# Last stage of a metaformer layer: the whole residual on VectorE, four statistics rows, weight pieces and centred gating weights

## The reference

```python
def conv(x, ...):                                  # x here is _ln_c(x)
    xn = layer_norm(x, norm_a, norm_b)
    left = (xn @ Wl + bl) * sigmoid(xn @ Wlg + blg)
    right = (xn @ Wr + br) * sigmoid(xn @ Wrg + brg)
    out_gate = sigmoid(xn @ Wog + bog)
    out = einsum('bkjd,bkid->bijd', left, right) / n
    out = layer_norm(out, on_a, on_b) * out_gate
    return out @ Wo + bo

def ffn(x, gate_w, gate_b, weight1, weight2):      # x here is _ln_t(t)
    logits = einsum('bsd,ed->bse', x, gate_w) + gate_b         # 64 experts
    probs = softmax(logits, axis=1)                            # over the tokens
    topv, topi = the 8 largest of each expert, and their tokens
    pooled = sum over the 8 of x[topi] * topv
    out = gelu([pooled, 1] @ weight1) then [., 1] @ weight2    # per expert
    return zeros.at[topi].add(out * topv)

x = x + conv(_ln_c(x), ...)
t = t + ffn(_ln_t(t), ...)
```

## Time and profile before

| | |
|---|---|
| median of 3 runs | 3088.07 us (3087.18 to 3091.25) |
| the profiled execution | 3078.97 us |
| its span in the profile | 3077.0 us |
| TensorE, VectorE, ScalarE, GpSimd busy over the span | 84%, 79%, 77%, 61% |
| last stage | about 1885 to 2953 us |

### The profile page before, as it was taken

How to read it: one execution, slowest core, us unless ns; L and a number is a source line. 1 busy time by engine, 2 the same in 40 slices (tenths; PEclk the granted TensorE clock), 3 DMA queues, 4 the chain that set the end, 5 groups by cost and what they waited for, 6 DMA issues and landing times.

```text
span 3077.0 us, 66113 instructions
## 1 busy us (share of the span) xinstructions
PE 2588.5 (84%) x14998; PEld 2145.9 (70%) x15070; DVE 2428.7 (79%) x4824; ACT 2363.5 (77%) x4284; POOL 1889.3 (61%) x2343
## 2 busy tenths in 40 slices
PE   7999999999999989989998984777777777777735
PEld 6888888888888878888988983555555555555523
DVE  6777777777777769999999996778777787787862
ACT  6888888888888877887878872888778787787850
POOL 8888888888888860000000003888788887887842
PEclk9999999999999999999999996999999999999967
DMA  5777777777777769999999985888888888888836
GB/s 199 270 267 268 267 270 273 270 269 269 267 268 268 270 256 318 333 327 325 343 330 325 332 295 185 301 309 307 297 300 309 303 299 298 309 309 297 303 139 202
DMA packets 281154, 873.00 MB, mean 284 GB/s; under 512 B 29223, under 2 KB 81602, under 8 KB 281122
## 3 DMA queue, kind: packets, MB, share of 16 engines
q1 hardware_dynamic: 272322, 855.31, 77.2%
q10 hardware_dynamic: 8448, 16.78, 1.6%
q0 software_dynamic: 352, 0.53, 0.2%
HBM read 492.97 MB, written 379.52 MB: 284 GB/s over the span
## 4 chain that ended last, share of the span: by engine, by line
PE 43%; DMA 17%; issue 14%; POOL 12%; DVE 5%; ACT 4%; SPq 2%; POOLq 1%; ACTq 0%; another core or an unknown queue 0%; DVEq 0%
PE banks L1267 32%; DMA arena<-left_d 11%; POOL rs L693 5%; DMA statrow<-stat_d 5%; POOL arena L664 4%; PE banks L1256 4%; PE banks L1335 3%; ACT arena L809 2%; PE banks L1301 1%; ACT work L879 1%; DVE left_parts L1006 1%; PE banks L1326 1%; PE banks L1336 1%; SPq L475 1%; DVE arena L1014 1%
## 5 line engine op out<-in xcount | busy, mean ns | idle before, releaser
L1267 PE MATMUL banks<-x_parts,w_parts 128*128 128x512 f32 x4320 | 1068.3, 399 | 0.8 <-POOL x_parts L626 0.8
L1267 PEld LDWEIGHTS banks<-x_parts,w_parts 128*128 128x128 f32 x4320 | 791.9, 189 | 162.9 <-POOL x_parts L626 1.2
L1301 PE MATMUL banks<-left_parts,right_parts 128*128 128x384 f32 x3456 | 629.3, 341 | 67.2 <-ACT arena L810 56.8
L1301 PEld LDWEIGHTS banks<-left_parts,right_parts 128*128 128x128 f32 x3456 | 606.2, 191 | 90.5 <-issue 86.0
L957 DVE SCALAR_TENSOR_TENSOR arena<-banks,cols,arena 128x512 f32<-128x512 f32 x576 | 406.6, 747 | 255.7 <-ACT arena L775 252.3
L879 ACT ACTIVATE work<-arena,nmr,rs 128x128 f32<-128x128 f32 x1152 | 458.9, 482 | 151.9 <-POOL nmr L695 145.5
L659 POOL COPY rcol<-late 128x8 f32 (+1 forms) x144 | 28.4, 197 | 722.3 <-ACT late L825 722.3
L664 POOL TENSOR_TENSOR arena<-arena,work 128x512 f32<-128x512 f32 x288 | 359.7, 1270 | 163.1 <-DVE arena L1063 161.9
L1335 PE MATMUL banks<-wo_sb,arena 128*128 128x128 f32 x2304 | 413.3, 309 | 0.1
L1335 PEld LDWEIGHTS banks<-wo_sb,arena 128*128 128x128 f32 x2304 | 373.6, 200 | 29.4 <-issue 1.8
L626 POOL TENSOR_TENSOR x_parts<-xn,x_parts 128x512 fp32r<-128x512 f32 x288 | 372.2, 1292 | 6.6 <-ACT x_parts L763 6.6
(11 more groups left out here) (177 smaller groups left out, 4459.5 us busy)
## 6 DMA issues: line engine op xcount, KB each, us to landing
arena<-in_x_dram SPq DMA_DIRECT2D x144, 512.0 KB, 3.4
left_d<-arena SPq DMA_DIRECT2D x144, 512.0 KB, 2.6
right_d<-arena SPq DMA_DIRECT2D x144, 512.0 KB, 3.4
gate_d<-arena SPq DMA_DIRECT2D x144, 512.0 KB, 4.2
arena<-right_d SPq DMA_DIRECT2D x128, 576.0 KB, 5.8
arena<-left_d SPq DMA_DIRECT2D x128, 576.0 KB, 6.8
mixed_d<-arena SPq DMA_DIRECT2D x128, 576.0 KB, 4.2
work<-mixed_d SPq DMA_DIRECT2D x144, 512.0 KB, 4.2
```

The lines of the kernel that those rows point to most:

```text
L1267: last = nc.tensor.matmul(ps[2 + k][:, :], w_parts[:, wq, k], x_parts[:, xq, b, c], start=((wq, xq) == TERMS[0]), stop=((wq, xq) == TERMS[ ...
L1301: last = nc.tensor.matmul(ps[NT * b + t][:, 0:GRID], lr_parts[RIGHT][:, rq, b, k, t * P:(t + 1) * P], lr_parts[LEFT][:, lq, b, k], start=( ...
```

## The change

- Residual: VectorE's `residual` now does both halves, eight operations. `scale_rest` on ScalarE and `residual_rest` on GpSimd are gone, with their semaphores; `store_result` waits for VectorE alone.
- Statistics rows: `statrow` loses its `b` dimension. A step's 18 rows lie at partitions 32r to 32r+17, r = s mod 4; `coef` is there four times. `outer` and `project` take these 18 partitions alone, with `tile_position=(BAND * r, 0)`. The loads run three steps ahead and wait for `project(s-4)` by their own step's number. SyncE and TensorE loop in fours (`quads`), and in SyncE's step the load of the statistics stands first.
- Weight pieces: `load_w1` issues one load of 0.5 MB at each of 28 cuts of ScalarE's loop, and four after it.
- Centred gating weights: each expert's mean over the channels is subtracted from `gate_nat` before the transpose. The logits then need no mean of the tokens: `normalise` becomes `x * rs`, and `minus` (L1092) and `nmr` (L695) go.
- Small ones: the sum of the exponents goes straight to `csum` (`keep_sum` is gone), `keep` copies two steps at once, and `exponentials` moves to the head of ScalarE's step.

The diff, cut:

```diff
+def quads(engine, steps, body, drain=0):
+
+    last = steps // 4 - 1
+    body(0)
+    with engine.Fori(1, last) as j:
+        body(j)
+    for j in range(last, steps // 4 + drain):
+        body(j)
...
-            def load_parts(i, b):
-                s = 2 * i + b
-                sp.wait_ge(s_z3, mark(2, s - 2, 2))
+            def load_parts(j, r):
+                s = 4 * j + r
+                if not isinstance(j, int) or j > 0:
+                    sp.wait_ge(s_z3, mark(2, s - 4, 2))
                 settle(sp, s_tick_sp)
-                sp.dma_start(statrow[0:KR, b], stat_r[s].broadcast_to([PARTS, 2 * PARTS, 2 * CHUNK])).then_inc(s_sin[b], 16)
+                sp.dma_start(statrow[BAND * r:BAND * r + KR], stat_r[s].broadcast_to([PARTS, 2 * PARTS, 2 * CHUNK])).then_inc(s_sin[r], 16)
...
-                        keep(*shifted(i, b, -4))
+                        if b:
+                            keep(i - 2)
...
-            def residual_rest(i, b):
-                pool.wait_ge(s_x3[b], 16 * (i + 1))
-                pool.wait_ge(s_zr, mark(1, 2 * i + b, 1))
-                half = late_arena[:, 1, b, 1]
-                nc.gpsimd.tensor_tensor(half, half, wv[:, 2, b, 1], ALU.add).then_inc(s_ra, 1)
...
             def load_w1(n):
-                for j in range(2 * n, 2 * n + 2):
-                    act.dma_start(w1_sb[:, j], w1_view[j]).then_inc(s_w1, 16)
+                j, first = n // 2, BANDS // 2 * (n % 2)
+                some = slice(first, first + BANDS // 2)
+                act.dma_start(w1_sb[:, j, some], w1_view[j, :, some]).then_inc(s_w1, 16)
...
-                        last = nc.scalar.activation(ys[:, b, h, c], summed[:, b, h, c], ACT.Identity,
-                                                    bias=nmr[:, b, k:k + 1], scale=rs[:, b, k:k + 1])
+                        last = nc.scalar.activation(ys[:, b, h, c], summed[:, b, h, c], ACT.Copy, scale=rs[:, b, k:k + 1])
...
-            cuts = [lambda n=n: load_w1(n) for n in range(WLOADS - 1)]
+            cuts = [lambda n=n: load_w1(n) for n in range(4 * (WLOADS - 1))]
...
+            link(nc.vector.tensor_reduce(gsum[:, :], gate_nat[:, :], AXX, ALU.add))
+            link(nc.vector.tensor_scalar(gsum[:, :], gsum[:, :], 1.0 / DIM, None, ALU.mult))
+            nc.vector.tensor_scalar(gate_nat[:, :], gate_nat[:, :], gsum[:, :], None, ALU.subtract).then_inc(s_gmean, 1)
...
+                for h in range(2):
+                    dve.wait_ge(s_z3, mark(2, s, h + 1))
+                    for c in range(TILES):
+                        k = TILES * h + c
+                        last = nc.vector.scalar_tensor_tensor(out=summed[:, b, h, c], in0=ps[2 + h][:, c * P:(c + 1) * P],
+                                                              scalar=rcol[:, b, k:k + 1], in1=xs[:, b, h, c],
+                                                              op0=ALU.mult, op1=ALU.add)
+                    last.then_inc(s_r3, 1)
...
-                    nc.tensor.matmul(ps[h][:, :], coef[:, 0, :], statrow[:, b, h, :], start=True, stop=True).then_inc(s_c3, 1)
...
+                    nc.tensor.matmul(ps[h][:, :], coef[rows, 0, :], statrow[rows, h, :], start=True, stop=True,
+                                     tile_position=(BAND * r, 0)).then_inc(s_c3, 1)
...
-                        last = nc.tensor.matmul(ps[2 + h][:, tok], statrow[:, b, h, tok], coef[:, 1, :], start=False, stop=True)
+                        last = nc.tensor.matmul(ps[2 + h][:, tok], statrow[rows, h, tok], coef[rows, 1, :], start=False, stop=True,
+                                                tile_position=(BAND * r, 0))
```

More of the change, by code:

```diff
@@ L86, in pairs, with shifted4, in_range4, halves_of @@
         body(i)
+def quads(engine, steps, body, drain=0):
[5 more added lines that the diff above has]
+        body(j)
+def shifted4(j, r, k):
+    return j + (r + k) // 4, (r + k) % 4
+def in_range4(j, r, k, steps):
+    return not isinstance(j, int) or 0 <= 4 * j + r + k < steps
+def halves_of(j, r):
+    return 2 * j + r // 2, r % 2
 def build(nc, x, norm_a, norm_b, Wl, bl, Wr, br, Wlg, blg, Wrg, brg, Wog, bog, on_a, on_b, Wo, bo,
@@ L351, in build @@
         s_x3 = [sem(f"s_x3{b}") for b in range(2)]
-        s_sin = [sem(f"s_sin{b}") for b in range(2)]
+        s_sin = [sem(f"s_sin{r}") for r in range(BANDS)]
         s_rc = sem("s_rc")
@@ L537, in _ @@
             sp.wait_ge(s_stst, 16 * 2 * PARTS)
-            load_parts(0, 0)
-            load_parts(0, 1)
-            pairs(sp, STEPS, stage3, drain=1)
+            for r in range(3):
+                load_parts(0, r)
+            quads(sp, STEPS, stage3, drain=1)
             w2_view = weight2[:, 0:HIDDEN, :].rearrange("(g j) (p c) n -> j p g (c n)", g=BANDS, c=HC)
@@ L593, in _ @@
             alone(nc.gpsimd.memset(pick_row[:, :, :], -1.0))
-            alone(nc.gpsimd.memset(statrow[:, :, :, :], 0.0))
+            alone(nc.gpsimd.memset(statrow[:, :, :], 0.0))
             alone(nc.gpsimd.memset(coef[:, :, :], 0.0))
@@ L714, in _ @@
             gate(0, 0)
-            pairs(pool, STEPS, stage3, drain=3, lead=3)
+            pairs(pool, STEPS, stage3, drain=2)
             for b in range(2):
@@ L900, in _ @@
                 act.wait_ge(s_ost[b], 16 * (STEPS // 2))
-            load_w1(WLOADS - 1)
+            for n in range(4 * (WLOADS - 1), 4 * WLOADS):
+                load_w1(n)
             act.wait_ge(s_nm, 1)
@@ L1354, in logits, with stage3 @@
                                      start=True, stop=True).then_inc(s_l3, 1)
-            def stage3(i):
-                for b in range(2):
-                    if in_range(i, b, 1, STEPS):
-                        outer(*shifted(i, b, 1))
-                    if in_range(i, b, 0, STEPS):
-                        project(i, b)
-                    if in_range(i, b, -3, STEPS):
-                        logits(*shifted(i, b, -3))
-                    if in_range(i, b, -2, STEPS):
-                        transposes3(*shifted(i, b, -2))
+            def stage3(j):
+                for r in range(4):
+                    if in_range4(j, r, 1, STEPS):
+                        outer(*shifted4(j, r, 1))
+                    if in_range4(j, r, 0, STEPS):
+                        project(j, r)
+                    if in_range4(j, r, -3, STEPS):
+                        logits(*halves_of(*shifted4(j, r, -3)))
+                    if in_range4(j, r, -2, STEPS):
+                        transposes3(*halves_of(*shifted4(j, r, -2)))
             pe.wait_ge(s_rtc, NT * NT)
-            pe.wait_ge(s_coef, 16 * PARTS)
+            pe.wait_ge(s_coef, 16 * PARTS * BANDS)
             pe.wait_ge(s_setup, 3)
             outer(0, 0)
-            pairs(pe, STEPS, stage3, drain=2)
-            pe.wait_ge(s_r3, mark(1, STEPS - 1, 1))
-            pe.wait_ge(s_zr, mark(1, STEPS - 1, 1))
+            quads(pe, STEPS, stage3, drain=1)
+            pe.wait_ge(s_r3, mark(2, STEPS - 1, 2))
             pe.wait_ge(s_p3, mark(2, STEPS - 1, 2))
```

121 lines of the change are left out of this document (42 added, 79 removed).

## The result

| | before | after |
|---|---|---|
| median | 3089.52 us (3087.18 to 3091.25, 4 runs) | 3338.14 us (3321.36 to 3346.42, 4 runs) |
| ratio | | 1.0798 (1.0752 to 1.0845) |
| span of the profiled execution | 3077.0 us | 3319.6 us |

What follows compares the result with a forecast made beforehand. Bound: the late statistics load, 7.385 us per step. TensorE's 5.2 plus 1.7, plus 0.05, gives 6.95: -62.2 us over 143 steps, start +1.5, profiled time 3018.3, plus 9.1 to the median: 3027.4 us; range 2994 to 3120.

Steps and rivals of the forecast that it cites:

- The ring: Last stage: statistics load waits for project(s), next outer for the load; 7.5 us a turn, mean 7.385; early loads free it.
- D: Rival: statistics load still held behind the result's store in SyncE's order; 3082 to 3096 us; 0.06 including near no change.
- VectorE's 6.75: VectorE's own time per step in the last stage after taking the whole residual: 6.02 - 0.35 + 1.04, about 6.75 us.
- the 0.05 in the sum: Last stage: 0.05 us per step added for TensorE and VectorE now and then waiting for one another.
- Rival B: Row groups cost TensorE nothing, pace is VectorE's 6.75: 2999 us; lower end of the forecast's 0.52, given little.
- The price of a change: TensorE, last stage: 0.10 us per change of array shape, bounds 0 and 0.16; seventeen more per step, 1.7 us.
- rival A: Changes of shape are dear on TensorE: 3215 us with bare weight loads, 3100 with gaps alone; 0.28 above pace 7.43.
- Lighter engines: Last stage: GpSimd falls from 6.18 to about 4.5 us busy per step, ScalarE from 5.85 to about 4.7.
- The exponent's wait for the maximum: Head of ScalarE's step: exponent waits for GpSimd's negated maximum, 3.4 us after VectorE begins; covered, priced nothing.
- Weight pieces: ScalarE's queue, last stage: 28 loads of 0.5 MB for 14 of 1 MB; gain already in the new pace.
- rival C: DMA engines cap at 310 to 315 GB/s, pace 7.2: 3063 us; 0.14 with rival A between 7.1 and 7.34.
- The start: Kernel start: centring the gating weights delays TensorE's start by three VectorE operations and a transpose, about 1.5 us once.

Runs made afterwards that it cites:

- e7: Kernel before with only four buffers for the statistics rows, loaded three steps ahead, all 128 rows read: 3003.53 us, ratio 0.9722.
- e10: e1 with the statistics load put back late, at the end of SyncE's step and two steps ahead: 3147.58 us, ratio 1.0187.
- e1: Changed kernel with the statistics matmuls reading all 128 partitions again, from four buffers side by side: 3001.33 us, ratio 0.971.
- e5: e1 with the statistics matmuls and outer on the first 64 rows: 3059.11 us, ratio 0.9886.
- e6: e1 with the statistics matmuls and outer on rows 0 to 17: 3337.83 us, ratio 1.0788.
- e12: e8 with the exponent moved from the end of ScalarE's step to between scaling and normalise: 2928.66 us, ratio 0.9486.
- e8: e7 with the weights loaded in 28 pieces of 0.5 MB in place of 14 of 1 MB: 3005.96 us, ratio 0.9739.
- e4: e1 with each statistics matmul of the projection issued as two of 64 columns over all 128 partitions: 3013.98 us, ratio 0.974.
- e11: e1 with the residual's second half put back on ScalarE and GpSimd, the exponent behind that scaling: 2897.16 us, ratio 0.9369.
- e3: Changed kernel with the projection reordered so two narrow matmuls stand together, 8 changes of shape in place of 16: 3057.07 us, ratio 0.989.
- e2: Kernel before with only outer and the projection's statistics matmuls cut from 128 to 18 partitions: 3509.17 us, ratio 1.1339.

## Why the prediction was wrong, point by point

- **The ring, and that one edit frees it.** Right. L1319 waits for the statistics row twice in the whole trace, 11.3 us together and 9.9 of them at the stage's start; D is out, and e7 and e10 show the ring from both sides.
- **VectorE's 6.75.** Nearly right: without the changes of shape (e1) the pace is 6.94, VectorE 0.94 busy. It is busy 659.79 / (700 / 6.94) = 6.54 us of it, and of its 40 us idle 36 are for its own results. So the 0.2 missing is not waiting in turn, as the 0.05 in the sum was meant: one step of the earlier trace rows was read for the mean. Rival B said 2999 by a pace of 6.75, and e1, where changes cost nothing, has 3001; but that agreement is luck. With e1's pace of 6.94 the same sum gives 3026. Of the 25 us between, 11 are a stage that happened to start earlier (1886.3 against 1897.5), 3.5 a shorter tail, and most of the rest the 9.1 that the sum adds from the profiled execution to the median, which e1 does not show (3000.54 and 3001.33).
- **The price of a change: a term that was too small.** I took 0.10, the row L1336 to L1353 of the earlier trace rows, and set aside the 0.16 of the other. Measured at full clock: 0.12, near the mean of the two. In the sum 17 x 0.12 = 2.04 in place of 1.7 makes TensorE 7.24 and the forecast about 3070 to 3076. e5, which has just this, had a pace of 7.26 and ran at 3059. By this term alone the change would still have been a small gain. Every step in and every step out costs, but an in and an out are a pair, and the pair of rows gave 0.26 where I counted 0.20.
- **The clock: the step that failed.** The sum, the forecast and both numbers of rival A took every matmul at the full clock of the earlier trace rows, and put nothing, without a reason, for a lower one. The runs showed a mean clock of 0.74 in its place, and a pace of 9.16. From e5's 3059 to e6's 3338 it is the clock alone, nine tenths of the miss. Rival A named the right engine and the right cause, but not this price: its 3215 came from weight loads that would be bare, which no row shows, and its 3100 from the gaps. That one mechanism costs first a gap and then the clock stood in no row of before: the fall in the earlier trace rows comes with TensorE idle more than half of the time. In another of that trace TensorE had waited 4.41 us for its statistics rows. The clock is 0.74 from 2546 to 2548 us, while TensorE is idle, and 0.50 from 2548 to 2552, while it works again:

```profile
2548.18 1.03 PE L1326 MATMUL banks<-statrow,coef 128*128 128x512 bf16 x2 [4.41 <-DMA statrow<-stat_d]
```

  The Trainium skill (TensorE: Matmul & The Clock Gate, HAM oscillation) tells of a low clock as the price of idle gaps between matmuls. The trace of before agrees; that of the changed kernel shows a fall that this does not cover, a clock of 0.74 with no idle time recorded in 900 us, and the 0.12 us at a change are not enough to explain it, since e5 has them too and keeps 1.00. For the changes themselves the trace agrees with the rule of the Trainium skill cited in the prediction, that changing the tiling mode drains TensorE (TensorEngine Tiling (Array Packing), Key Properties): each costs 0.12 us.
- **Lighter engines.** GpSimd 449.22 / (900 / 9.164) = 4.57 us per step (4.5 was said), ScalarE 4.28 (4.7): `normalise` without its bias takes 0.39 an operation, not the 0.48 that I left it at. Neither decided.
- **The exponent's wait for the maximum.** It is there, 313.7 us of 900 in ScalarE, and hidden, as said. But where it stands matters in a kernel that is not bound by TensorE: e12 gained 77 us by it. I saw the edit as cover for a wait and not as what frees TensorE's bank.
- **Weight pieces.** No gain of their own (e8), as the text said of them once the rows come early.
- **Transfers, rival C.** Out at this pace: e4 moves 322 GB/s with the DMA engines at 0.92. If there is a ceiling in this stage, it is not below the 363 of e11.
- **The start.** The first product starts at 23.3 us in place of 22.7: +0.6, not +1.5. TensorE was waiting 4.93 us for `w_parts`, and 2.4 of these became cover for the later transpose.

What stays open is what it is in the alternation that brings the clock down. 18 rows with 8 changes in a projection keep 0.93, 64 rows or 64 columns with 16 keep 1.00, 32 rows or fewer with 16 fall to 0.73. No run here separates the part of the rows from that of the changes, or tries a number of rows between 32 and 64.

## What to carry to other kernels

Price a change of TensorE's array shape at the full round trip, in and out (here 0.24 us at full clock), and don't let narrow matmuls alternate with full ones in a busy loop: pad to all 128 rows with zeros, which keeps the pair at 0.33 us and the clock at 1.00 here (e1, 3001 us). Two narrow ones in a row bring only part of it (e3, 3057 us). When an operation's duration enters a sum, check the clock at which it was read, and ask if the change keeps that clock. And take a bundle apart: here a loss of 337 us hid 88 us of gain, and beside these lay an edit that costs about 100 us once the others let the kernel run.

## What the runs showed of the chip that was not expected

- The granted clock falls from 2.4 to 1.2 GHz with no idle time of TensorE in the record, when matmuls of 32 rows or fewer alternate with full ones (0.73 to 0.74 in the mean, and 0.67 in e2); 64 rows in the same places keep 1.00, though the rows from 18 on hold only zeros (e5).
- A change of array shape costs 0.12 us at 2.4 GHz whether it goes to 18, 32 or 64 rows (pairs of 0.58, 0.57 and 0.58, against 0.33), and 0.10 to 64 columns (groups of 0.59 with one matmul more, against 0.38).
- 363 GB/s of loads and stores in the mean over 700 us, with the DMA engines at 0.98 (e11).
